# Cross-attention and feed-forward layer on one core: the sums' reciprocals on VectorE, the softmax's high part one step later, the last eight groups divided ahead too

## The chip, the cores and the metric

The kernel runs on one core of one Trainium2 chip. The metric is device time in microseconds (us) of one execution. The kernel before was timed three times: 1075.79, 1072.92 and 1074.25 us, median 1074.25 us. One more execution was recorded by the hardware profiler, and all rows below come from that one.

## The reference

Sixteen sequences of 128 tokens (2048 tokens, width 1024) pass through one cross-attention layer and one gated feed-forward layer, all in float32:

```python
x = x + xattn(layernorm(x), ctx, ctx, w_q, w_k, w_v, w_out, mask)
x = x + ffn(layernorm(x), w12, b12, w3, b3)

# xattn: 32 query heads of 32 columns, 8 key/value groups (4 query heads share one group)
scores = einsum('bghnd,bgsd->bghns', query, key) / 32 ** 0.5
scores = where(mask, scores, finfo.min)
out = einsum('bghns,bgsd->bghnd', softmax(scores), value) @ w_out.T

# ffn
x1, x2 = split(x @ w12.T + b12)
y = (silu(x1) * x2) @ w3.T + b3
```

## The kernel before

**Pieces.** TensorE multiplies 16-bit numbers, so each float32 operand is split into a high float16 part (written by ScalarE, `*_hi`) and a low part, the rest (written by VectorE or GpSimd, `*_lo`). A product is three matmuls: high by high, high by low, low by high. The engines are named in the profile as PE (TensorE), ACT (ScalarE), DVE (VectorE), POOL (GpSimd) and SP (the queue that issues the DMAs). Each engine runs its instructions strictly in the order in which they are written, and waits on semaphores.

**Blocks, steps and groups.** The 16 sequences are taken as 8 blocks of U = 2 sequences, and the attention of a block as 8 key/value groups. A group g = 0 to 63 is thus one key/value group of one pair of sequences: 8 score tiles of 128 by 128 (u = 0, 1 and four heads j each). The main loop is `for t in 1..8, for s in 0..7`: step (t, s) works on group g = 8(t-1)+s, and every engine has a loop of that shape of its own. Beside the group, a step holds a unit or two of other work: the q, k and v projections of block t, the turning (transposing) of the next x rows at s = 7, the output projection of block t-2 at s = 3 to 6, the splitting of the next block's context on POOL at s = 0 and 1 (`split_ctx`, L928), the look at later weights' maxima on DVE (`max_of`, L1729). At t = 8 the first feed-forward products (`hidden`) and POOL's splitting of w12 take the place of the projections.

**A group's way.** PE: `scores(g)` (L1457). DVE: `mask_scores(g)` (L1884) adds the mask, finds each row's extreme and writes e, 8 instructions of L1895; after each four it counts up `neg_max_done`. ACT: `exps(g, u)` (L1201), four exponentials for each u. For a group in `NORMED` (8 to 47) they also leave each row's sum in p_sum, and P is divided by its sums before it is split: by DVE for the two first groups of a block (`by_vector`, L308; `norm_prob` in the DVE program, L1908: a reciprocal L1912 and a product L1915 for each u), by POOL for the other six (`by_pool`, L313; `norm_prob` of POOL, L975: a scaling L979, a power of -1 L981 and a product L985 for each u). Then ACT writes the high part of both u in one instruction (`prob_hi`, L1213, L1222), POOL the low part in two (`prob_lo`, L969, L972; in groups outside 12 to 47 the u = 0 half is DVE's, L1903). SP turns both parts with a DMA transpose (`turn_prob`, L727), and PE multiplies them with v (`weigh`, L1474) three steps after the scores. For groups in NORMED that is the tiled form (L1487 to L1493): 32 columns of v as weights, four heads side by side in the array, and the result is already transposed. For the other groups (0 to 7 and 48 to 63) P is not divided, `weigh` runs two steps after the scores in the plain form (L1497 to L1501) with a column of ones that gives the sum, DVE divides the result (`divide`, L1920) and PE turns it (`turn_attn`, L1424).

**What ties the steps.** e is kept for two groups only (index g % 2). So `mask_scores(g)` waits (L1890 to L1893) until both parts of group g-2 are split, and `scores(g+1)` waits until `mask_scores(g)` has read its bank (L1465). Products go through five PSUM banks in turn (three at the beginning and end), and each product waits until the bank's last content was read (`begin`, L1381). In the order before, ACT's step is `exps(g, 0)`, the high parts of the step's first unit and of the attention result g-3, `exps(g, 1)`, the second unit's high part, `prob_hi(g)` (L1309 to L1339). POOL's step is `prob_lo(g-1)`, `norm_prob(g)`, then its splits (L990 to L1007). DVE's step is L2082 to L2127.

## Time and profile before

| quantity | value |
|---|---|
| time, median of 3 | 1074.25 us |
| the profiled execution's own time | 1076.37 us |
| its span, first to last instruction | 1074.6 us |
| PE busy | 1026.1 us (95%) |
| DVE busy | 670.4 us (62%) |
| POOL busy | 644.7 us (60%) |
| ACT busy | 473.2 us (44%) |
| mean granted clock of PE, share of 2.4 GHz | 0.979 |

1.8 us of the profiled execution lie outside its span. A busy share is an average over all stages: the attention takes about the first 600 us, the feed-forward products the rest. The profile counts a matmul busy until its modelled end, and matmuls overlap, so what a group of short matmuls costs is read from start to start. "PEclk" 1.00 is 2.4 GHz and 0.50 is 1.2 GHz. A row of idle time such as "[3.10 <-ACT arena_rows L1298]" says how long the engine had waited before that instruction and whose work ended the wait.

### The profile page before, as it was taken

How to read it: one execution, taken by the hardware profiler on the slowest of the kernel's cores; microseconds unless marked ns; L12 is line 12 of the kernel's file. 1: busy time of each engine (PE TensorE's matmuls, PEld its weight loads, DVE VectorE, ACT ScalarE, POOL GpSimd, SP SyncE). 2: the span in 40 equal slices, each digit the busy share in tenths (PEclk: the TensorE clock that was granted, in tenths of full speed). 3: DMA queues.
4: the chain of work that ended last, by engine and by line, in shares of the span. 5: the costliest groups of instructions: out<-in, count | busy, mean ns of one | idle time of the engine just before them, and what ended most of it. 6: DMA issues, size and time to landing. Idle time of an engine off the chain costs nothing.

```text
span 1074.6 us, 22142 instructions
## 1 busy us (share of the span) xinstructions
PE 1026.1 (95%) x8320; PEld 683.5 (64%) x8320; DVE 670.4 (62%) x2040; ACT 473.2 (44%) x1303; POOL 644.7 (60%) x657
## 2 busy tenths in 40 slices
PE   8898899998979989989999999999999999999998
PEld 7786757766658557677755544444444788468853
DVE  6889976767677667777856523735766255635431
ACT  5767566656566556666566511123432011301110
POOL 2769877987978879878985879226862201203000
PEclk8998999998999989989999999999999999999999
DMA  9569676897798788969994552397649731774201
GB/s 370 212 171 190 152 193 166 175 249 198 193 219 217 206 210 176 254 173 237 231 255 79 136 218 94 134 271 255 225 164 226 267 113 55 196 238 135 80 30 49
DMA packets 230779, 199.13 MB, mean 185 GB/s; under 512 B 177040, under 2 KB 187280, under 8 KB 225808
## 3 DMA queue, kind: packets, MB, share of 16 engines
q1 hardware_dynamic: 230672, 197.72, 67.1%
q8 instruction: 66, 1.08, 0.4%
q14 instruction: 41, 0.34, 0.1%
HBM read 119.04 MB, written 35.65 MB: 144 GB/s over the span
## 4 chain that ended last, share of the span: by engine, by line
PE 61%; POOL 19%; ACT 5%; DVE 4%; issue 4%; DMA 1%; SPq 1%; DVEq 0%; POOLq 0%; ACTq 0%
PE bank_dense L1411 38%; PE bank_spare L1411 7%; PE bank_score L1567 6%; PE bank_spare L1567 5%; POOL arena_attn L972 5%; POOL arena_attn L981 4%; POOL arena_attn L985 4%; PE bank_av L1567 3%; POOL arena_in L908 2%; ACT arena_attn L1207 2%; POOL arena_in L904 2%; ACT arena_attn L1222 2%; DVE arena_attn L1895 1%; POOL arena_in L906 1%; PE bank_score L1468 1%
## 5 line engine op out<-in xcount | busy, mean ns | idle before, releaser
L1411 PE MATMUL bank_dense<-arena_rows,arena_in 128*128 128x256 f16 (+1 forms) x1272 | 176.1, 296 | 1.6 <-POOL arena_in L908 0.9
L1411 PE MATMUL bank_dense<-arena_attn,arena_rows 128*128 128x512 f16 x768 | 166.4, 379 | 0.0
L1411 PEld LDWEIGHTS bank_dense<-arena_rows,arena_in 128*128 128x128 f16 x1272 | 122.1, 98 | 44.5 <-DVE arena_in L1743 1.3
L1895 DVE CUSTOM_DVE_ANT_0 arena_attn<-bank_score,arena_in 128x128 f32<-128x128 f32 x512 | 143.5, 344 | 0.7 <-PE bank_score L1468 0.5
L1411 PEld LDWEIGHTS bank_dense<-arena_attn,arena_rows 128*128 128x128 f16 x768 | 75.2, 98 | 90.1
L972 POOL TENSOR_TENSOR arena_attn<-arena_attn 128x512 f16<-128x512 f32 x89 | 103.3, 1177 | 46.8 <-ACT arena_attn L1222 46.8
L1207 ACT ACTIVATE arena_attn<-arena_attn,arena_in 128x128 f32<-128x128 f32 x320 | 123.7, 390 | 16.5 <-DVE arena_in L1895 16.5
L1411 PE MATMUL bank_dense<-arena_out,arena_attn 128*128 128x512 f16 x576 | 127.8, 379 | 0.5 <-DVE arena_attn L1937 0.5
L1222 ACT ACTIVATE arena_attn<-arena_attn 128x1024 f16<-128x1024 f32 x64 | 67.5, 1055 | 108.5 <-POOL arena_attn L985 96.8
L1411 PEld LDWEIGHTS bank_dense<-arena_out,arena_attn 128*128 128x128 f16 x576 | 55.5, 98 | 64.0 <-DVE arena_attn L1937 0.6
L1411 PE MATMUL bank_spare<-arena_rows,arena_in 128*128 128x256 f16 (+1 forms) x648 | 87.7, 292 | 0.0
L1411 PE MATMUL bank_dense<-arena_out,arena_in 128*128 128x512 f16 x384 | 83.0, 379 | 0.0
L908 POOL TENSOR_TENSOR arena_in<-arena_in 128x512 f16<-128x512 f32 x62 | 77.1, 1243 | 5.0
L1210 ACT ACTIVATE arena_attn<-arena_attn,arena_in 128x128 f32<-128x128 f32 x192 | 60.8, 391 | 34.1 <-DVE arena_in L1895 33.8
L1411 PEld LDWEIGHTS bank_spare<-arena_rows,arena_in 128*128 128x128 f16 x648 | 62.3, 98 | 19.8
L2000 DVE SCALAR_TENSOR_TENSOR arena_out<-bank_dense,small,arena_out 128x256 f32<-128x256 f32 x64 | 27.9, 478 | 74.9 <-PE bank_dense L1411 74.9
L1411 PEld LDWEIGHTS bank_dense<-arena_out,arena_in 128*128 128x128 f16 x384 | 37.6, 98 | 45.3
L1411 PE MATMUL bank_dense<-arena_in 128*128 128x256 f16 x456 | 64.4, 308 | 1.5 <-DVE arena_in L1750 1.4
L985 POOL TENSOR_TENSOR arena_attn<-arena_attn 128x512 f32<-128x512 f32 x60 | 62.4, 1039 | 4.7
L981 POOL TENSOR_TENSOR arena_attn<-arena_attn 128x4 f32<-128x4 f32 x60 | 62.1, 1035 | 5.0
L918 POOL TENSOR_TENSOR small<-small 128x1 f32<-128x1 f32 x32 | 20.2, 633 | 72.9 <-DVE small L1784 72.9
L1207 ACT ACTIVATION_READ_ACCUMULATOR arena_attn<-arena_attn,arena_in 128x1 f32 x320 | 60.6, 189 | 0.0
(237 smaller groups left out, 1942.1 us busy)
## 6 DMA issues: line engine op xcount, KB each, us to landing
arena_rows<-x SPq DMA_DIRECT2D x32, 512.0 KB, 5.4
arena_in<-w_scratch SPq DMA_DIRECT2D x64, 256.0 KB, 3.0
arena_attn<-q_scratch SPq DMA_DIRECT2D x48, 256.0 KB, 4.3
arena_rows<-w_t SPq DMA_DIRECT2D x12, 1024.0 KB, 6.4
arena_rows<-ctx_t SPq DMA_DIRECT2D x8, 1024.0 KB, 5.9
q_scratch<-arena_attn SPq DMA_DIRECT2D x16, 512.0 KB, 4.6
x_scratch<-arena_rows SPq DMA_DIRECT2D x16, 512.0 KB, 4.1
arena_out<-x_scratch SPq DMA_DIRECT2D x16, 512.0 KB, 5.7
```

The source lines that it names most:

```text
L904: pool.tensor_tensor(buf, src, spread, ALU.mult).then_inc(s_pool, 1)
L908: pool.tensor_tensor(lo, buf, hi, ALU.subtract).then_inc(ready, 1)
L972: ins = pool.tensor_tensor(p_split[:, g % 2, u, 1], e[:, g % 2, u], p_split[:, g % 2, u, 0], ALU.subtract)
L981: pool.tensor_tensor(inv_pool[:, u], inv_pool[:, u], minus_one.broadcast_to([P, HPG]), ALU.pow)\
L985: ins = pool.tensor_tensor(heads, heads, inv_pool[:, u].rearrange("p (j o) -> p j o", o=1) .broadcast_to([P, HPG, SEQ]), ALU.mult)
L1207: ins = act.activation(head, head, ACT.Exp, bias=neg_max[:, g % 2, h:h + 1], scale=-1.0, accum_out=p_sum[:, g % 2, u, j:j + 1])
L1210: ins = act.activation(head, head, ACT.Exp, bias=neg_max[:, g % 2, h:h + 1], scale=-1.0)
L1222: act.activation(p_split[:, g % 2, :, 0], e[:, g % 2], ACT.Copy).then_inc(s_phi, 1)
L1411: ins = pe.matmul(dst, lhs(a, c), rhs(b, c), start=(c == chunks[0] and n == 0), stop=(c == chunks[-1] and n == 2))
L1567: ins = pe.matmul(seven(v, j), weights[:, a, P * c:P * c + P], rows[:, b, c], start=(c == 0 and n == 0), stop=(c == 3 and n == 2))
L1895: ins = dve.tensor_tensor_reduce(out=e[:, g % 2, h // HPG, SEQ * (h % HPG):SEQ * (h % HPG) + SEQ], in0=B_SCORE[:, SEQ * h:SEQ * h + SEQ], ...
L2000: ins = dve.scalar_tensor_tensor(out=cols, in0=bank("y", f, q)[:, 256 * k:256 * k + 256], scalar=c_ffn[:, 2 * h + k:2 * h + k + 1], in1=co ...
```

## The change

Four things change.

1. The reciprocals of all divided groups are made by DVE, in a new helper `inv_sums(g, u)`: a scaling of p_sum by 1/P_SCALE and a reciprocal, each on 128 by 4 numbers and with a wait between them. POOL's `norm_prob(g, u)` is only the product. Where DVE divides, its own product becomes a `tensor_tensor` behind the same two small instructions.
2. For POOL's groups the second half's reciprocal, the second half's product and the high part move to the next step: DVE calls `inv_sums(g-1, 1)` at the start of step g ahead of `mask_scores(g)`, POOL's step is `norm_prob(g-1, 1)`, `prob_lo(g-1)`, `norm_prob(g, 0)`, and ACT calls `prob_hi(g-1)` behind `exps(g, 0)`.
3. Groups 56 to 63 join NORMED, all divided by DVE. At t = 8 DVE's `norm_prob(g)` stands ahead of `first_half_read` and `attn_lo`.
4. With that, groups 56 to 63 are weighed in the tiled form, three steps behind their scores, and lose `divide` and `turn_attn`.

```diff
-NORMED = range(8, 48)
+NORMED = [*range(8, 48), *range(56, 64)]

 def by_vector(g):
-    return g in NORMED and g % GROUPS < 2
+    return g in NORMED and (g % GROUPS < 2 or g >= 56)

 def by_pool(g):
-    return g in NORMED and g % GROUPS >= 2
+    return g in NORMED and g % GROUPS >= 2 and g < 56

+def inv_count(g, u):
+    return U * normed_count(g - 1) + u + 1
...
# POOL
-            def norm_prob(g):
+            def norm_prob(g, u):
                 n = normed_count(g - 1, by_pool)
-                for u in range(U):
-                    pool.wait_ge(s_exp, 2 * g + u + 1)
-                    pool.tensor_scalar(inv_pool[:, u], p_sum[:, g % 2, u], 1 / P_SCALE, None, ALU.mult).then_inc(s_pinv, 1)
-                    pool.wait_ge(s_pinv, 2 * (U * n + u) + 1)
-                    pool.tensor_tensor(inv_pool[:, u], inv_pool[:, u], minus_one.broadcast_to([P, HPG]), ALU.pow)\
-                        .then_inc(s_pinv, 1)
-                    pool.wait_ge(s_pinv, 2 * (U * n + u) + 2)
-                    heads = e[:, g % 2, u].rearrange("p (j n) -> p j n", j=HPG)
-                    ins = pool.tensor_tensor(heads, heads, inv_pool[:, u].rearrange("p (j o) -> p j o", o=1)
-                                             .broadcast_to([P, HPG, SEQ]), ALU.mult)
-                ins.then_inc(s_pnorm, 1)
+                pool.wait_ge(s_vinv, inv_count(g, u))
+                heads = e[:, g % 2, u].rearrange("p (j n) -> p j n", j=HPG)
+                pool.tensor_tensor(heads, heads, inv[:, g % 2, u].rearrange("p (j o) -> p j o", o=1)
+                                   .broadcast_to([P, HPG, SEQ]), ALU.mult).then_inc(s_pnorm, 1)
...
-                    if GROUPS * (t - 1) + s > PLO_ALONE:
-                        prob_lo(GROUPS * (t - 1) + s - 1)
-                    if by_pool(GROUPS * (t - 1) + s):
-                        norm_prob(GROUPS * (t - 1) + s)
+                    g = GROUPS * (t - 1) + s
+                    if by_pool(g - 1):
+                        norm_prob(g - 1, 1)
+                    if g > PLO_ALONE:
+                        prob_lo(g - 1)
+                    if by_pool(g):
+                        norm_prob(g, 0)
...
# ACT
                     exps(g, 0)
+                    if by_pool(g - 1):
+                        prob_hi(g - 1)
...
-                    prob_hi(g)
+                    if not by_pool(g):
+                        prob_hi(g)
...
# PE, the steps behind the loop
-                turn_attn(NG - 11 + s)
-                if s < 10:
-                    weigh(NG + s - 10)
+                weigh(NG - 11 + s)
...
# DVE
+            def inv_sums(g, u):
+                dve.wait_ge(s_exp, 2 * g + u + 1)
+                dve.tensor_scalar(sums[:, g % 2, u], p_sum[:, g % 2, u], 1 / P_SCALE, None, ALU.mult).then_inc(s_vsum, 1)
+                dve.wait_ge(s_vsum, inv_count(g, u))
+                dve.reciprocal(inv[:, g % 2, u], sums[:, g % 2, u]).then_inc(s_vinv, 1)
...
                 for u in range(U):
-                    dve.wait_ge(s_exp, 2 * g + u + 1)
-                    dve.reciprocal(inv_vector[:, u], p_sum[:, g % 2, u]).then_inc(s_vinv, 1)
-                    dve.wait_ge(s_vinv, U * n + u + 1)
+                    inv_sums(g, u)
+                    dve.wait_ge(s_vinv, inv_count(g, u))
                     heads = e[:, g % 2, u].rearrange("p (j n) -> p j n", j=HPG)
-                    ins = dve.scalar_tensor_tensor(out=heads, in0=heads, scalar=P_SCALE,
-                                                   in1=inv_vector[:, u].rearrange("p (j o) -> p j o", o=1)
-                                                   .broadcast_to([P, HPG, SEQ]), op0=ALU.mult, op1=ALU.mult)
+                    ins = dve.tensor_tensor(heads, heads, inv[:, g % 2, u].rearrange("p (j o) -> p j o", o=1)
+                                            .broadcast_to([P, HPG, SEQ]), ALU.mult)
...
+                    if by_pool(g - 1):
+                        inv_sums(g - 1, 1)
                     if g >= 3:
                         divide(g - 3)
                     mask_scores(g)
...
+                    if by_vector(g) and t == NB:
+                        norm_prob(g)
                     if t == NB and s in H_AT:
                         first_half_read(0, H_AT[s])
                     if g >= 3:
                         attn_lo(g - 3)
-                    if by_vector(g):
+                    if by_vector(g) and t < NB:
                         norm_prob(g)
+                    elif by_pool(g):
+                        inv_sums(g, 0)
```

What stands in a row on POOL at step s = 3 of block t = 4 (group 27) before: L972 is `prob_lo(26)`, L979, L981 and L985 are `norm_prob(27)`, L918 and L925 are small work for a row's scale.

```order
L972 TENSOR_TENSOR arena_attn<-arena_attn 128x512 [waits prob_hi_done]
L972 TENSOR_TENSOR arena_attn<-arena_attn 128x512
L979 TENSOR_SCALAR arena_attn<-arena_attn 128x4 [waits exp_done]
L981 TENSOR_TENSOR arena_attn<-arena_attn 128x4 [waits pool_inv_sum_done]
L985 TENSOR_TENSOR arena_attn<-arena_attn 128x512 [waits pool_inv_sum_done]
L979 TENSOR_SCALAR arena_attn<-arena_attn 128x4 [waits exp_done]
L981 TENSOR_TENSOR arena_attn<-arena_attn 128x4 [waits pool_inv_sum_done]
L985 TENSOR_TENSOR arena_attn<-arena_attn 128x512 [waits pool_inv_sum_done]
L918 TENSOR_TENSOR small<-small 128x1 [waits var_done]
L925 TENSOR_TENSOR arena_in<-arena_in,small 128x1 [waits root_done]
```

And now (L980 is the product, L973 `prob_lo(26)`, L921 and L928 the small work):

```order
L980 TENSOR_TENSOR arena_attn<-arena_attn 128x512 [waits inv_sum_of_prob_done]
L973 TENSOR_TENSOR arena_attn<-arena_attn 128x512 [waits prob_hi_done]
L973 TENSOR_TENSOR arena_attn<-arena_attn 128x512
L980 TENSOR_TENSOR arena_attn<-arena_attn 128x512 [waits inv_sum_of_prob_done]
L921 TENSOR_TENSOR small<-small 128x1 [waits var_done]
L928 TENSOR_TENSOR arena_in<-arena_in,small 128x1 [waits root_done]
```

Four small instructions are gone, and the second product of group 26 stands ahead of its low part.

ACT at the same place before, from the end of step s = 2 through step 3 (L1207 an exponential, L1222 `prob_hi`, L1177 the attention result's high part, L1191 that of k):

```order
L1222 ACTIVATE arena_attn<-arena_attn 128x2x512 [waits even_prob_turned,prob_normed_by_pool]
L1207 ACTIVATE arena_attn<-arena_attn,arena_in 128x128 [waits neg_max_done]
L1207 ACTIVATE arena_attn<-arena_attn,arena_in 128x128 x3
L1177 ACTIVATE arena_attn<-bank_dense2 128x256 [waits dense_done]
L1207 ACTIVATE arena_attn<-arena_attn,arena_in 128x128 [waits neg_max_done]
L1207 ACTIVATE arena_attn<-arena_attn,arena_in 128x128 x3
L1191 ACTIVATE arena_in<-bank_spare 128x256 [waits dense_done,k_spilled_0]
L1222 ACTIVATE arena_attn<-arena_attn 128x2x512 [waits odd_prob_turned,prob_normed_by_pool]
```

And now (L1204, L1219, L1174 and L1188 are the same):

```order
L1204 ACTIVATE arena_attn<-arena_attn,arena_in 128x128 [waits neg_max_done]
L1204 ACTIVATE arena_attn<-arena_attn,arena_in 128x128 x3
L1219 ACTIVATE arena_attn<-arena_attn 128x2x512 [waits even_prob_turned,prob_normed_by_pool]
L1174 ACTIVATE arena_attn<-bank_dense2 128x256 [waits dense_done]
L1204 ACTIVATE arena_attn<-arena_attn,arena_in 128x128 [waits neg_max_done]
L1204 ACTIVATE arena_attn<-arena_attn,arena_in 128x128 x3
L1188 ACTIVATE arena_in<-bank_spare 128x256 [waits dense_done,k_spilled_0]
L1204 ACTIVATE arena_attn<-arena_attn,arena_in 128x128 [waits neg_max_done]
```

`prob_hi(26)` stood ahead of the first exponentials of group 27; now it stands behind them and ahead of the attention result's high part. `prob_hi(27)` is no longer in this step.

DVE at step s = 4 of t = 8 (group 60), between two runs of `mask_scores`, before (L1905 `prob_lo`, L1952 the output projection's sum, L1937 the attention result's low part, L1925 and L1927 `divide`):

```order
L1895 ISA arena_in 128x1
L1895 ISA arena_attn,arena_in<-bank_score,arena_in 128x128
L1895 ISA arena_in 128x1
L1895 ISA arena_attn,arena_in<-bank_score,arena_in 128x128
L1895 ISA arena_in 128x1
L1895 ISA arena_attn,arena_in<-bank_score,arena_in 128x128
```

And now (L1908, L1910 and L1917 are the scaling, the reciprocal and the product for each u, L1903, L1953 and L1935 as L1905, L1952 and L1937 before):

```order
L1893 ISA arena_in 128x1
L1893 ISA arena_attn,arena_in<-bank_score,arena_in 128x128
L1893 ISA arena_in 128x1
L1893 ISA arena_attn,arena_in<-bank_score,arena_in 128x128
L1893 ISA arena_in 128x1
L1893 ISA arena_attn,arena_in<-bank_score,arena_in 128x128
L1893 ISA arena_in 128x1
L1893 ISA arena_attn,arena_in<-bank_score,arena_in 128x128
L1893 ISA arena_in 128x1
L1893 ISA arena_attn,arena_in<-bank_score,arena_in 128x128
```

Six instructions, two of them on 512 columns, stand where `divide` had two.

## Rows read from the trace of the kernel before

**Rows 1.** DVE by line and shape: busy us, mean ns | idle before.

```profile
L1731 DVE TENSOR_REDUCE arena_in<-arena_rows 128x1 f32<-128x2048 f32 x19 | 43.3, 2279 | 14.5 <-DMA arena_rows<-w_t 14.5
```

**Rows 2.** Busy time by engine, PEclk, DMA; stretches t = 2, 3, 4, 7, and 8 (s = 3 to 6).

```profile
112.90:185.30 72.40, 65.53 (x646) 46.99 (x642) 55.96 (x202) 42.99 (x162) 56.36 (x63) 0.98 0.67 164
185.30:256.80 71.50, 65.56 (x660) 46.76 (x661) 49.66 (x190) 43.18 (x163) 59.89 (x68) 0.95 0.87 214
256.80:328.40 71.60, 65.64 (x661) 46.80 (x661) 49.75 (x190) 43.20 (x163) 59.87 (x68) 0.95 0.84 209
...
471.60:539.20 67.60, 67.13 (x712) 50.66 (x713) 54.10 (x227) 42.39 (x106) 59.48 (x64) 1.00 0.90 220
...
574.10:599.90 25.80, 25.80 (x239) 14.59 (x236) 19.67 (x89) 13.90 (x37) 18.10 (x19) 1.00 0.48 103
```

**Rows 3.** The chain that ended last, 255 to 327 us: start, us, what.

```profile
284.50 2.28 POOL arena_attn L972 x2
...
287.17 1.05 POOL arena_attn L981
...
288.29 1.04 POOL arena_attn L985
...
291.90 1.07 ACT arena_attn L1222
...
293.03 2.27 POOL arena_attn L972 x2
```

**Rows 4.** Who waited for whom, whole span: us in total, times, longest.

```profile
ACT arena_attn L1222 <- POOL arena_attn L985: 96.8, 25, 6.7
...
POOL arena_attn L972 <- ACT arena_attn L1222: 46.8, 32, 6.8
```

**Rows 5.** PE's instructions in order of time at t = 3, s = 7: start, us, [idle before].

```profile
248.53 0.66 PE L1420 MATMUL bank_spare<-arena_in,arena_rows 128*128 128x128 f32 x4 [3.10 <-ACT arena_rows L1298]
250.80 1.12 PE L1420 MATMUL bank_spare<-arena_in,arena_rows 128*128 128x128 f32 x4 [1.61 <-DVE v_low L1865]
```

**Rows 6.** POOL by line and shape: busy us, mean ns | idle before.

```profile
L981 POOL TENSOR_TENSOR arena_attn<-arena_attn 128x4 f32<-128x4 f32 x60 | 62.1, 1035 | 5.0
...
L979 POOL TENSOR_SCALAR arena_attn<-arena_attn 128x4 f32<-128x4 f32 x60 | 14.0, 233 | 16.4 <-ACT arena_attn L1207 13.2
```

**Rows 7.** DVE in order of time, t = 4: the first instruction of `mask_scores(24)` to (27).

```profile
257.94 0.35 DVE L1895 CUSTOM_DVE_ANT_0 arena_attn<-bank_score,arena_in 128x128 f32<-128x128 f32 x1
...
264.49 0.33 DVE L1895 CUSTOM_DVE_ANT_0 arena_attn<-bank_score,arena_in 128x128 f32<-128x128 f32 x1
...
271.53 0.33 DVE L1895 CUSTOM_DVE_ANT_0 arena_attn<-bank_score,arena_in 128x128 f32<-128x128 f32 x1
...
279.55 0.34 DVE L1895 CUSTOM_DVE_ANT_0 arena_attn<-bank_score,arena_in 128x128 f32<-128x128 f32 x1
```

**Rows 8.** DVE's small instructions in SBUF: duration min/median/max, ns.

```profile
L1880 DVE TENSOR_SCALAR arena_in<-arena_in,small x8: 221/223/1187, 60.8 to 539.6; 128x8 f32<-128x8 f32 x8
```

**Rows 9.** The same view of the reciprocal.

```profile
L1912 DVE RECIPROCAL arena_attn<-arena_attn x20: 159/168/178, 120.6 to 412.9; 128x4 f32<-128x4 f32 x20
```

**Rows 10.** DVE in order of time at t = 8, s = 6.

```profile
596.79 1.68 DVE L1905 TENSOR_TENSOR arena_attn<-arena_attn 128x512 f16<-128x512 f32 x1
```

**Rows 11.** POOL in order of time, the same moment.

```profile
596.76 1.16 POOL L908 TENSOR_TENSOR arena_in<-arena_in 128x512 f16<-128x512 f32 x1
```

**Rows 12.** The chain that ended last, 110 to 186 us: tiled `weigh`, four exponentials with sums.

```profile
152.40 0.45 PE bank_dense L1489 x24
...
180.60 1.54 ACT arena_attn L1207 x8
```

**Rows 13.** PE in order of time, t = 8: `turn_attn`, the first plain `weigh` matmul, `scores(63)`.

```profile
599.11 0.38 PE L1428 MATMUL bank_dense<-arena_in 128*128 128x128 f32 x2
599.33 0.18 PE L1497 MATMUL bank_av<-v_high,arena_attn 128*128 128x33 f16 x1
...
599.94 0.61 PE L1468 MATMUL bank_score<-arena_attn 96*128 96x128 f16 x8
```

More of the change, by code:

```diff
@@ L433, in xattn_ffn @@
         p_sum = part(arena_attn, 59, 1, F32)[:, 0:2 * U * HPG].rearrange("p (r u j) -> p r u j", r=2, u=U)
-        inv_pool = part(arena_attn, 60, 1, F32)[:, 0:U * HPG].rearrange("p (u j) -> p u j", u=U)
-        minus_one = part(arena_attn, 62, 1, F32)[:, 0:1]
-        inv_vector = part(arena_attn, 61, 1, F32)[:, 0:U * HPG].rearrange("p (u j) -> p u j", u=U)
+        sums = part(arena_attn, 60, 1, F32)[:, 0:2 * U * HPG].rearrange("p (r u j) -> p r u j", r=2, u=U)
+        inv = part(arena_attn, 61, 1, F32)[:, 0:2 * U * HPG].rearrange("p (r u j) -> p r u j", r=2, u=U)
         k_stack = part(arena_attn, 63, 4).rearrange("p (b g n) -> p b g n", b=2, g=4)
@@ L1214, in prob_hi @@
                 if by_pool(g):
-                    act.wait_ge(s_pnorm, normed_count(g, by_pool))
+                    act.wait_ge(s_pnorm, U * normed_count(g, by_pool))
                 elif by_vector(g):
```

8 lines of the change are left out of this document (2 added, 6 removed).

## The prediction

> **What bounds the kernel now.** The page's busy times, which stand in the table above, come first: PE is busy 1026.1 of 1074.6 us, so all that PE idles is 48.5 us. Then the busy times by block [rows 2]: blocks t = 3 to 6 take 71.5 or 71.6 us each (two of the four are shown, the others read alike), with PE busy 65.6 of them at a mean clock of 0.95. So PE idles 6.0 us in each, and 0.05 of lost clock is about 7 us at 1.2 GHz, whose busy part costs 2.6 to 3.4 us. A block in which PE never waited would take 71.6 - 6.0 - (2.6 to 3.4) = 62.2 to 63.0 us, and I take 62.6. What PE waits for is in the chain [rows 3]: it runs through POOL, not PE. In one step the low part of the group before (2.28 us, from 284.50), then twice the scaling, the power (1.05) and the product (1.04) with a wait of about 0.07 between them, then ACT's high part (1.07), then POOL's next low part at 293.03. That is 8.53 us a step, of which none can run beside another: POOL waits for ACT and ACT for POOL. The waits say the same from both sides [rows 4]: ACT sat 96.8 us until POOL's product, POOL 46.8 us until ACT's high part. PE's steps s = 3 to 6 last about as long, but at s = 0 to 2 PE is faster and POOL's two context splits slower, and the debt is paid at s = 7, where PE waits 3.10 us for an x row that ACT scaled too late (it stood behind `prob_hi`) and 1.61 us for v's low part behind the exponentials [rows 5]. The clock dips follow these waits.
>
> **What goes.** For each of 30 groups POOL loses two powers of 1.035 us and two scalings of 0.233 us [rows 6], with their waits 2.8 us a step, and ACT's 1.07 us leaves the loop since POOL no longer needs the high part of its own group in the same step. POOL is busy 59.9 us of a block [rows 2]; less 6 x 2 x 1.27 = 15.2 it is 44.7. POOL stops being a bound, except that at s = 0 and 1 its splits (two trios of instructions a step, some 6.7 us) still hold up the low part by which `mask_scores` two groups on is released.
>
> **What comes in its place: DVE and its ping-pong with ACT.** DVE now makes 12 pairs in a block for POOL's groups and four scalings for its own. The reciprocal has one price, 0.17 us [rows 9]. The scaling has none in the rows for 128 by 4; the nearest is L1880, a scaling of 128 by 8 in SBUF: 0.22 us in the median and 1.19 at most [rows 8]. The long ones began while POOL was at work. The same is seen at 596.79: DVE's subtraction from SBUF took 1.68 us, begun while POOL's L908 ran from 596.76 for 1.16 us, and so ended about half a microsecond after it [rows 10, 11]. So a scaling costs 0.25 to 1.2 us, a pair 0.45 to 1.4. Below 0.45 nothing speaks for it. I take 0.45 where POOL is waiting for this very pair (most second halves) and 0.8 to 0.9 elsewhere.
>
> The Trainium skill ("SBUF — State Buffer", Terms) says that DVE and GpSimd arbitrate for one port pair, and that "the loser fully blocks"; "GPSIMD Engine Reference" (Specifications) narrows it to DVE instructions in a two-port mode or with two SBUF inputs. The trace agrees: 1.68 us beside 1.16 us, and a reciprocal never above 0.178 us. By this rule the scaling was the wrong instruction to hand to DVE in s = 0 and 1, where POOL splits without a gap; the high end above is what it would give.
>
> Now the chain of DVE through a block, from the start of one `mask_scores` to the next. Before, it was 6.55, 7.04 and 8.02 us for s = 0 to 3 [rows 7], back to back. Now:
> - s 0 to 1: 6.55 + 0.96 (ACT's high part of group 7 of the block before now stands between the exponentials and all that DVE waits for, 1.07 less overlap [rows 3]) + two scalings, and a first product that meets POOL: 8.0 to 9.6, I take 9.0.
> - s 1 to 2: 7.04 + two scalings: 7.5 to 9.4, take 8.1.
> - s 2 to 3: 8.02 + two pairs: 8.9 to 10.8, take 9.2.
> - s 3 to 7, four intervals: none was back to back before. The interval 2 to 3 holds half of the mask, four exponentials (1.54 [rows 12]), the high and low parts behind them, a maximum (L1731, 2.28 us [rows 1]) and a row's statistics; steps 3 to 6 have only one of these two last. So 8.02 less about 2, plus the high part 0.96 and two pairs of 0.45 (to 0.9 for one): 6.9 to 7.9 without the low part that now waits behind the attention result (L1934, 0.3 to 0.4 more). I take 7.9 each, 31.6; 7.2 and 8.3 are the ends.
> - s 7 to 0: the same with four x halves, gather and block scales: 9.6 to 10.6, take 10.
> The sum is 34.0 + 28.8 = 62.8 at the low ends, 36.3 + 31.6 = 67.9 as taken, 40.4 + 33.2 = 73.6 at the high ends. PE's floor of 62.6 lies at or below all of them: the step is bound by DVE and ACT in turn. Since the takes lean to contention, and POOL is idle a third of the time, I set the block at 66.8, a little below the taken sum. That is 71.6 - 66.8 = 4.8 us, and in four blocks 19.2 us. PE then waits some 4 us a block in pieces of at most 2 us; block t = 2 lost 6.9 us of PE's time with a mean clock of 0.98 [rows 2], so I expect most of the dips to go.
>
> **Block t = 2** (72.4 us) is already DVE's at its first three steps: DVE is busy 56.0 us in it against 49.7 later [rows 2]. There each scaling lands on the path: 4 x 0.6 and two pairs, 3.5 us more; its s = 7 gets about 1.5 us shorter. Net +2.
>
> **Block t = 7** (67.6, PE busy 67.1) is PE's own and stays.
>
> **Block t = 8.** The tiled form costs 0.45 us a group [rows 12]. The plain one costs 599.94 - 599.33 = 0.61 and the turn 599.33 - 599.11 = 0.22 [rows 13], together 0.83. Saved: 8 x 0.38 = 3.0 us, since PE is the bound there (25.8 of 25.8 us at s = 3 to 6 [rows 2]). That PE's busy column gives far more to the plain form is only overlap. Against it: DVE at s = 3 to 6. It is busy 19.7 of 25.8 us, 4.9 a step [rows 2]. It loses `divide` (about 0.65) and gains two scalings, two reciprocals and two products of 512 columns, 0.7 to 1.3 each: 2 x (0.25 + 0.2 + 0.7) = 2.3 to 2 x (0.7 + 0.2 + 1.25) = 4.3. DVE's step becomes 6.6 to 8.6 us, against PE's 6.45 - 0.38 = 6.07. POOL splits w12 there nearly without gaps, so I take 8.3. `scores(g+1)` waits for `mask_scores(g)`, which now stands behind the products of group g-1: the first such wait is about 1, the next two 2.2 each, 5.4 us. Net +2.4, say +2. At s = 0 to 2 and 7 a step is over 11 us and hides it. The DMA transposes get a step more time.
>
> **Sum.** 1076.4 - 19.2 + 2 + 0 + 2 = 1061.2 for the profiled execution. It was 2.1 us above the median of the runs, so the same difference of -15.2 gives 1059.0 us.
>
> **Rivals.**
> - *DVE's additions stay hidden and PE is the bound.* For it: DVE was busy only 49.7 of 71.6 us, and its waits for ACT could absorb 12 pairs. Against: DVE's intervals at s = 0 to 3 were already back to back. Blocks of 63.5: -32; t = 2 at 0, t = 8 at 0: 1043. Chance 0.25.
> - *POOL and ACT keep the pace.* The low parts at s = 0 and 1 still stand behind the splits, the high part costs ACT's time ahead of each attention result, and blocks end at 69.5 us: -8.4 + 2 + 2: 1070. Chance 0.15.
> - *DVE becomes a worse bound than POOL was: slower.* One mechanism: each scaling and product waits for POOL's running instruction. If a pair costs 1.2 us on average instead of my 0.45 to 0.9, the 12 pairs alone add 4 to 6 us to the 67.9, its chain is 72, PE's waits at s = 7 stay over 3 us and the dips with them. It decides from a mean of about 1.2 us a pair; the price is +0.5 a block, +5 at t = 2, +6 at t = 8: 1074.25 + 2 + 5 + 6 = 1087. The skill's rule above is what would make it so. Against: POOL waits for the pair in most steps, and then its port is free. Chance 0.11.
> - *The change does not do what it says.* The order shows that the power and scalings are gone from POOL and the high part moved, so only its timing is open: 0.04, no change.
>
> **How the numbers follow.** The forecast has 0.45. Its own range, with blocks of 65 to 68.5, is 1051 to 1067. Down to 1040 it takes in most of the first rival, up to 1073 the second and a little of the third. This kernel can be told from no change at 0.3%, 3.2 us. Faster than 1071.0: 0.45 + 0.25 + 0.13 of the second = 0.83. Slower than 1077.5: 0.10 of the third. Within: the rest, 0.02 + 0.01 + 0.04 = 0.07.
>
> **What would show it.** Right: blocks t = 3 to 6 of 65 to 68.5 us; POOL busy about 45 in each; ACT's wait for POOL's product nearly gone and DVE's waits for ACT's high parts grown; scalings of 0.2 to 1.2 us, mean 0.4 to 0.6; PE's waits now for `mask_scores` (L1893) at s = 2 to 4 and for low parts at s = 7; PEclk 0.99 or 1.00 there; at t = 8, s = 3 to 6, a step of 7.5 to 8.5 us, ended by `mask_scores`. Wrong: blocks under 64 (DVE hid it), blocks over 70 with POOL's low part ahead of each `mask_scores` (second rival), or a mean pair over 1.2 us (third).

## The result and the profile after

The changed kernel takes 1114.59 us (median of 4 runs, 1113.54 to 1117.02) against 1074.65 us before: 1.0376 times as long, 95% interval 1.0354 to 1.0399. I had forecast 1059.0. It is slower, on the other side of no change, and 41.6 us beyond the range's upper end of 1073.

The profiled executions differ by 1115.2 - 1074.6 = 40.6 us of span. By the starts of `scores` the difference lies here: block t = 2 +0.3 us; blocks t = 3 to 6, 77.6, 78.3, 78.2 and 76.4 instead of 71.5 or so, +24.2 together; block t = 7 +3.8; from the start of t = 8 to the end 547.8 instead of 535.4, +12.4. Busy times of the whole, the granted clock in 40 slices, and the chain by engine:

```profile
PE 1036.3 (93%) x8304; PEld 679.9 (61%) x8304; DVE 734.9 (66%) x2212; ACT 478.2 (43%) x1367; POOL 571.3 (51%) x536
...
PEclk8999899898898989999999999999999999999999
...
PE 52%; DVE 20%; ACT 7%; DMA 7%; issue 4%; POOL 3%; SPq 2%; ACTq 0%; DVEq 0%; POOLq 0%
```

The same by stretches, as in [rows 2]: t = 2, 3, 5, 7, and t = 8 from s = 4 on.

```profile
112.70:185.50 72.80, 66.03 (x649) 47.51 (x644) 60.28 (x229) 43.03 (x162) 40.08 (x39) 0.95 0.60 149
185.50:263.10 77.60, 68.87 (x661) 47.66 (x661) 58.81 (x219) 43.21 (x163) 44.41 (x44) 0.91 0.79 199
341.40:419.60 78.20, 68.18 (x660) 47.41 (x659) 58.74 (x218) 43.02 (x163) 44.39 (x44) 0.91 0.76 192
496.00:567.40 71.40, 67.69 (x714) 50.75 (x714) 54.73 (x229) 42.06 (x106) 60.01 (x65) 1.00 0.90 220
612.00:650.00 38.00, 31.96 (x266) 15.16 (x265) 35.84 (x107) 19.81 (x80) 25.91 (x25) 0.91 0.37 84
```

POOL's column did what was forecast: 44.4 us a block where it was 59.9. But no engine of these blocks is full. PE idles 8.7 us of block t = 3 and 10.0 of t = 5, and its clock is 0.91 in both, not the 0.99 that I expected. At t = 8 it is DVE that is full: 35.8 of 38.0 us. Who waited for whom, as in [rows 4], and in a second fence DVE's maxima with the idle time before them, as in [rows 1]:

```profile
POOL arena_attn L973 <- ACT arena_attn L1219: 101.8, 37, 7.5
...
POOL arena_attn L980 <- DVE arena_attn L1910: 77.3, 31, 7.9
...
ACT arena_attn L1219 <- DVE arena_attn L1917: 55.7, 18, 4.6
```

```profile
L1729 DVE TENSOR_REDUCE arena_in<-arena_rows 128x1 f32<-128x2048 f32 x19 | 43.1, 2270 | 24.2 <-DMA arena_rows<-w_t 24.2
```

ACT's wait for POOL's product, 96.8 us in [rows 4], is gone; POOL now waits for DVE's reciprocal instead. And DVE stands 24.2 us in front of its maxima until a load of weights has landed, where it stood 14.5 before. The chain of waits shows what that means. At t = 5, from step 5 into step 7:

```profile
393.71 0.96 ACT arena_attn L1219
394.74 2.28 POOL arena_attn L973 x2
397.07 1.79 SPq L736
398.92 7.14 DMA arena_rows<-w_t
406.08 2.29 DVE arena_in L1729
408.37 0.33 DVE arena_attn L1863
408.96 0.35 DVE arena_attn L1893
```

Read it downwards: P's high part, one step late, lets POOL make the low parts; these release SyncE's transpose of P (L736); only behind that does SyncE's queue issue the load of the next weights, 7.14 us; then DVE takes their maximum, and behind that in its row stand what `mask_scores` (L1893) and all of the next step need. The same place in SyncE's queue, step 3 of t = 5, after and (second fence) before the change; the blocks begin at 341.4 and 328.4 us, so the context load leaves 38.4 us into the block instead of 33.0, and the weight load right behind it:

```profile
366.98 12.72 SPq L736 DMA_TRANSPOSE arena_attn<-arena_attn  x2
379.75 0.57 SPq L698 DMA_DIRECT2D arena_rows<-ctx_t  x1
380.38 0.42 SPq L760 DMA_DIRECT2D arena_rows<-w_t  x1
```

```profile
349.86 11.49 SPq L733 DMA_TRANSPOSE arena_attn<-arena_attn  x2
361.41 0.57 SPq L695 DMA_DIRECT2D arena_rows<-ctx_t  x1
362.04 0.42 SPq L757 DMA_DIRECT2D arena_rows<-w_t  x1
```

### The profile page after: what moved, and what is told of

The parts are those of the page before. It is cut to its first block, busy times and chain, and to the rows that moved or that the text cites. A ratio compares the mean times of both kernels' runs of the same rounds, so it can differ in the third digit from the quotient of the medians.

```text
span 1115.2 us, 22218 instructions
## 1 busy us (share of the span) xinstructions
PE 1036.3 (93%) x8304; PEld 679.9 (61%) x8304; DVE 734.9 (66%) x2212; ACT 478.2 (43%) x1367; POOL 571.3 (51%) x536
## 4 chain that ended last, share of the span: by engine, by line
PE 52%; DVE 20%; ACT 7%; DMA 7%; issue 4%; POOL 3%; SPq 2%; ACTq 0%; DVEq 0%; POOLq 0%
PE bank_dense L1411 33%; PE bank_score L1567 5%; PE bank_spare L1567 5%; DVE arena_attn L1893 5%; PE bank_spare L1411 5%; DMA arena_rows<-w_t 5%; ACT arena_attn L1204 4%; PE bank_av L1567 3%; DVE arena_in L1729 2%; DVE arena_attn L1908 2%; DVE arena_attn L1917 2%; POOL arena_attn L973 2%; SPq L736 2%; DVE arena_attn L1903 1%; DVE arena_attn L1863 1%
## 5 line engine op out<-in xcount | busy, mean ns | idle before, releaser
L1204 ACT ACTIVATE arena_attn<-arena_attn,arena_in 128x128 f32<-128x128 f32 x384 | 148.8, 391 | 129.0 <-DVE arena_in L1893 129.0
L1411 PE MATMUL bank_dense<-arena_rows,arena_in 128*128 128x256 f16 (+1 forms) x1272 | 180.2, 300 | 1.8 <-POOL arena_in L911 1.0
L973 POOL TENSOR_TENSOR arena_attn<-arena_attn 128x512 f16<-128x512 f32 x89 | 102.9, 1173 | 101.8 <-ACT arena_attn L1219 101.8
L1893 DVE CUSTOM_DVE_ANT_0 arena_attn<-bank_score,arena_in 128x128 f32<-128x128 f32 x512 | 143.8, 346 | 1.4 <-PE bank_score L1468 0.8
L1411 PE MATMUL bank_dense<-arena_out,arena_attn 128*128 128x512 f16 x576 | 136.1, 396 | 4.4 <-DVE arena_attn L1935 4.4
L1411 PEld LDWEIGHTS bank_dense<-arena_out,arena_attn 128*128 128x128 f16 x576 | 57.3, 101 | 74.9 <-issue 10.9
L980 POOL TENSOR_TENSOR arena_attn<-arena_attn 128x512 f32<-128x512 f32 x60 | 63.3, 1055 | 77.3 <-DVE arena_attn L1910 77.3
L1219 ACT ACTIVATE arena_attn<-arena_attn 128x1024 f16<-128x1024 f32 x64 | 67.1, 1048 | 55.8 <-DVE arena_attn L1917 55.7
L911 POOL TENSOR_TENSOR arena_in<-arena_in 128x512 f16<-128x512 f32 x62 | 77.9, 1256 | 5.0
L1204 ACT ACTIVATION_READ_ACCUMULATOR arena_attn<-arena_attn,arena_in 128x1 f32 x384 | 72.7, 189 | 0.0
L1411 PE MATMUL bank_dense<-arena_in 128*128 128x256 f16 x456 | 59.4, 293 | 1.5 <-DVE arena_in L1748 1.4
L921 POOL TENSOR_TENSOR small<-small 128x1 f32<-128x1 f32 x32 | 19.9, 622 | 78.7 <-DVE small L1782 78.7
L1468 PE MATMUL bank_score<-arena_attn 96*128 96x128 f16 x512 | 40.1, 222 | 20.8 <-DVE arena_in L1893 19.4
L1729 DVE TENSOR_REDUCE arena_in<-arena_rows 128x1 f32<-128x2048 f32 x19 | 43.1, 2270 | 24.2 <-DMA arena_rows<-w_t 24.2
```

The costliest lines, as they stand in the source:

```text
L911: pool.tensor_tensor(lo, buf, hi, ALU.subtract).then_inc(ready, 1)
L973: ins = pool.tensor_tensor(p_split[:, g % 2, u, 1], e[:, g % 2, u], p_split[:, g % 2, u, 0], ALU.subtract)
L980: pool.tensor_tensor(heads, heads, inv[:, g % 2, u].rearrange("p (j o) -> p j o", o=1) .broadcast_to([P, HPG, SEQ]), ALU.mult).then_inc(s_ ...
L1204: ins = act.activation(head, head, ACT.Exp, bias=neg_max[:, g % 2, h:h + 1], scale=-1.0, accum_out=p_sum[:, g % 2, u, j:j + 1])
L1219: act.activation(p_split[:, g % 2, :, 0], e[:, g % 2], ACT.Copy).then_inc(s_phi, 1)
L1411: ins = pe.matmul(dst, lhs(a, c), rhs(b, c), start=(c == chunks[0] and n == 0), stop=(c == chunks[-1] and n == 2))
```

## The experiments

Before was measured anew beside each group of kernels: 1073.9 to 1075.3 us. All times are medians; a kernel's "gain" is against the changed kernel's 1114.6.

**Loads first.** In SyncE's steps:

```
+ if 3 <= t < 7 and s == 3: load_look(look_at(t, 4), w3_t[t - 3])
+ if 3 <= t < 7 and s == 5: load_look(look_at(t, 6), w12_t[2 * (t - 3) + 1])
+ if t < NB - 1 and s == 3: load_ctx(t + 1)
  if g >= 1: turn_prob(g - 1)
  ...
- (the same three, from behind turn_prob)
```

> The changed kernel with one thing moved in SyncE's order: at steps 3 and 5 of blocks 3 to 6 the loads of the weights that VectorE takes maxima of (L760 in the changed kernel), and at step 3 the load of the next context (L698), are issued ahead of that step's transposes of P instead of behind them. Theory A (VectorE's row of work is the bound of every block from 2 on, and 5.4 to 6.6 us of it a block are waits of L1729 for these loads, which leave late because the transposes ahead of them in SyncE's queue wait for the P low parts that now come later): the waits of L1729 fall from 24.2 us in all to under 8, the two long intervals between the starts of mask_scores (12.2 to 13.3 us from step 4 to 5, 10.0 to 10.4 from step 6 to 7) fall to 8 to 9, blocks 3 to 6 from 78 to 72 or 73 us, the whole to 1090 to 1096 us. Theory B (the wait only stands where another would stand: POOL's second product, the matmul rows at half clock, or a transfer that isn't faster for leaving earlier): under 6 us gained, 1109 to 1115 us.

1091.01 us, 1.0159 of before (1.0135 to 1.0184): a gain of 23.6 us. L1729's wait for weights is 0.6 us in all, and blocks 3 to 6 take 70.6, 72.0, 71.3 and 72.1 us, a little below theory A's 72 or 73. Theory A holds. The edit moves the context load too, but no engine of the changed kernel waits for one, so the gain is that of the loads for the maxima. By place: blocks 3 to 6 are 24.4 us shorter, block t = 7 is 1.7 longer. Block t = 5 in four stretches, s = 0 to 2, 3, 4 to 6, 7:

```profile
326.80:348.60 21.80, 19.08 (x242) 16.06 (x241) 18.61 (x73) 12.32 (x48) 16.83 (x16) 1.00 0.85 224
348.60:361.20 12.60, 11.89 (x80) 6.28 (x81) 10.63 (x35) 6.99 (x32) 7.79 (x10) 0.73 0.96 277
361.20:387.70 26.50, 26.50 (x244) 16.30 (x243) 20.80 (x80) 16.08 (x60) 15.08 (x16) 1.00 0.83 189
387.70:398.10 10.40, 8.90 (x100) 7.38 (x98) 8.35 (x33) 8.29 (x26) 4.75 (x5) 1.00 0.60 148
```

The third row matters for the forecast: in steps 4 to 6 PE is busy 26.50 of 26.50 us at full clock. It needs 8.8 us for each of these steps, whatever DVE does. Most of what the block loses, it loses in steps 0 to 3: DVE's intervals of 8.9 us hold up `scores` at the start of step 3 by 2.5 us and the output projection behind it by 0.7, and then PE runs at a clock of 0.73 through step 3:

```profile
348.59 0.94 PE L1468 MATMUL bank_score<-arena_attn 96*128 96x128 f16 x8 [2.52 <-DVE arena_in L1893]
350.24 7.96 PE L1411 MATMUL bank_dense<-arena_out,arena_attn 128*128 128x512 f16 x24 [0.71 <-DVE arena_attn L1935]
```

**The last groups as before.** `NORMED` is again `range(8, 48)`, and behind the loop `turn_attn` and `weigh` as before the change.

> The changed kernel with groups 56 to 63 as before the change (no product on P, division after the weighting, turned attention); the rest of the change stays. It prices the part on groups 56 to 63. Theory A (its price is paid in block 8 alone: steps 3 to 6 there are set by VectorE at 9.5 us instead of TensorE's 6.45, and at step 3 TensorE waits 3.6 us for ScalarE, which stands behind VectorE's products): from the start of block 8 to the end the kernel comes back from 547.8 us to 535 to 538, the whole to 1101 to 1105 us. Rival (block 8 is late because the seven blocks before hand it a late start for its operands, whatever its groups do): the end part stays at 545 or more and the whole above 1111 us.

1102.75 us (1.0269, 1.0247 to 1.0290): a gain of 11.8. From the start of t = 8, at 565.0, to the end at 1100.4 it is 535.4 us again. Theory A holds. Blocks 3 to 6 stay at 76.2 to 78.3. The part on groups 56 to 63 costs what the end part lost. Where: DVE's row in step 5 of t = 8 of the changed kernel, and (second fence) POOL at that time.

```profile
621.12 1.02 DVE L1908 TENSOR_SCALAR arena_attn<-arena_attn 128x4 f32<-128x4 f32 x1
622.18 0.18 DVE L1910 RECIPROCAL arena_attn<-arena_attn 128x4 f32<-128x4 f32 x1
622.39 1.40 DVE L1917 TENSOR_TENSOR arena_attn<-arena_attn 128x512 f32<-128x512 f32 x1
623.71 0.57 DVE L1908 TENSOR_SCALAR arena_attn<-arena_attn 128x4 f32<-128x4 f32 x1
624.32 0.18 DVE L1910 RECIPROCAL arena_attn<-arena_attn 128x4 f32<-128x4 f32 x1
624.53 1.51 DVE L1917 TENSOR_TENSOR arena_attn<-arena_attn 128x512 f32<-128x512 f32 x1
```

```profile
620.96 1.16 POOL L911 TENSOR_TENSOR arena_in<-arena_in 128x512 f16<-128x512 f32 x1
622.20 1.04 POOL L907 TENSOR_TENSOR arena_in<-arena_in,small 128x512 f32<-128x512 f32 x1
623.31 0.95 POOL L909 CAST arena_in<-arena_in 128x512 f16<-128x512 f32 x1
624.34 1.15 POOL L911 TENSOR_TENSOR arena_in<-arena_in 128x512 f16<-128x512 f32 x1
```

The first scaling, of 128 by 4 numbers, ends at 622.14; POOL's L911 had ended at 622.12. The second ends at 624.28, POOL's L909 at 624.26. Each product ends 0.55 us after the POOL instruction that ran when it began. Two pairs and two products take 4.9 us here (621.12 to 626.04), so DVE's step is 9.5 us where PE needs 6.2 (step 4, in which it does not wait). At step 3 the products also hold up ACT, whose high part, table load and SiLU stand before the attention result that the output projection needs:

```profile
605.94 7.04 PE L1411 MATMUL bank_spare<-arena_out,arena_attn 128*128 128x512 f16 x24 [3.65 <-DVE arena_attn L1938]
```

After 3.65 us of idling the 24 matmuls run partly at the lower clock: 7.04 us, where the same 24 take 5.35 in the next step. The granted clock of the whole step is 0.85.

**No scaling.** In `inv_sums` the `tensor_scalar` goes and the reciprocal reads `p_sum`; the kernel leaves out the factor of 1/P_SCALE.

> The changed kernel without the scaling of the sums by 1/16384 (VectorE L1908 goes, 0.51 us a piece, 8.1 us a block by its 16); the reciprocals are taken of the sums themselves, so P goes into the weighting without its factor of 16384 and the output is too small by it in groups 8 to 47 and 56 to 63. The work is otherwise the same. Theory A (VectorE's row is the bound of blocks 2 to 6, so what leaves it leaves the block): 12 of the 16 pairs of a block stand in it at 0.5 us or more with a gap of 0.07, so blocks 3 to 6 lose 6 to 9 us each, block 2 some 3 to 5, block 8 some 4; the whole 1076 to 1086 us. Rival (the waits for the loads and for ScalarE fill what is freed): blocks lose 3 us or less, the whole 1098 to 1110 us.

1087.79 us (1.0125, 1.0104 to 1.0146): a gain of 26.8, near theory A but beyond its 1086 on the slow side. By place it is not as A had it: blocks 3 to 6 fall by only 3.1 to 4.6 us each, 14.9 together, and L1729's wait for weights grows to 35.4 us. DVE is earlier, SyncE's queue isn't, so part of the gain is handed to the loads. The end part, from 547.8 to 534.8, gave 13.0 where A had 4.

**Products in their own step.** GpSimd calls `norm_prob(g, 0)` and `norm_prob(g, 1)` behind `prob_lo(g - 1)`, ScalarE calls `prob_hi(g)` at the end of each step, VectorE `inv_sums(g, 1)` last in it.

> The changed kernel with the one-step delay undone and the reciprocals left on VectorE: GpSimd makes both products of a group in that group's step, ScalarE takes P's high part at the end of that step, VectorE makes the second reciprocal as the last thing of the step (the same place in its row but for one small instruction). Theory A (the delay matters only through what waits for P's low part: SyncE's transposes, and the loads behind them): the low parts come 2 to 4 us earlier in a step, the waits of L1729 for the loads fall from 24 us to 8 to 15, and the whole comes to 1095 to 1107 us. Theory C (the delay is what freed ScalarE: without it ScalarE waits for GpSimd's second product, which itself waits for VectorE's last instruction, and the exponentials of the next step stand behind that): blocks 3 to 6 grow by 3 us or more each, the whole 1125 us or more.

1102.06 us (1.0258, 1.0233 to 1.0283): a gain of 12.5. The loads' wait is 13.7 us, blocks 3 to 6 take 74.9 to 75.4. Theory A; C falls, though ACT again waits 94.4 us for POOL's product.

**Sums at stride 2.** `p_sum` and `sums` become `...[:, 0:4 * U * HPG]` rearranged with a last dimension of 2, of which element 0 is used.

> The changed kernel with the sums of P and the scaled sums laid out at every second element (stride 2) instead of side by side; nothing else differs. In the changed kernel the scaling L1908 of 128x4 numbers takes 0.16 us where GpSimd is idle and up to 1.12 us beside it, 0.51 us in the mean, while the reciprocal L1910 of the same size takes 0.17 to 0.18 us everywhere. Theory P (the scaling waits only because a contiguous tensor_scalar runs in a form that shares a port with GpSimd; spread elements take it out of that form): the scalings take 0.15 to 0.25 us each, blocks 3 to 6 lose 4 to 6 us each, the whole 1092 to 1101 us. Rival (the wait is that of any multiplication beside GpSimd, whatever its layout): the mean stays at 0.45 us or more, the whole 1110 to 1118 us.

1118.47 us (1.0416, 1.0394 to 1.0438): no gain, 3.9 us worse, and the cause stays open: blocks t = 3 to 5 read as in the changed kernel, but t = 6 takes 78.1 us instead of 76.4 and t = 7 74.2 instead of 71.4. The 66 scalings that begin while POOL works still take 0.64 us in the mean. So the wait is not one of the layout's side-by-side elements. The Trainium skill ("VectorE: DVE Perf Modes", What auto-detection actually checks) asks for unit steps only in the mode for 16-bit tensors, not in the two-port mode of a single source in SBUF; by that rule stride could change nothing, and the run agrees.

**A second reciprocal in the scaling's place.**

```
- dve.tensor_scalar(sums[:, g % 2, u], p_sum[:, g % 2, u], 1 / P_SCALE, None, ALU.mult).then_inc(s_vsum, 1)
+ dve.reciprocal(sums[:, g % 2, u], p_sum[:, g % 2, u]).then_inc(s_vsum, 1)
...
- dve.reciprocal(inv[:, g % 2, u], sums[:, g % 2, u]).then_inc(s_vinv, 1)
+ dve.reciprocal(inv[:, g % 2, u], p_sum[:, g % 2, u]).then_inc(s_vinv, 1)
```

The first result is not used, and the factor of 1/P_SCALE is left out.

> The changed kernel with each scaling of the sums on VectorE replaced by a second reciprocal of the same 128x4 numbers, with the same wait behind it; the count of VectorE's instructions, their order and their semaphores are unchanged, and P goes into the weighting without its factor of 16384 in groups 8 to 47 and 56 to 63. It tells the instruction apart from what it waits for. Theory P (a reciprocal doesn't stand still for GpSimd's running instruction, as L1910 doesn't at 0.18 us everywhere, and the scaling does, at 0.51 us in the mean): all of the new first instructions take 0.18 us, so 16 x 0.33 = 5.3 us a block leave VectorE's row; without the instruction and its gap (0.58 us a pair) the kernel measured 1087.8 us, 26.8 below the changed kernel, so this one gains 0.33/0.58 of that, some 15 us: 1094 to 1103 us. Rival N (the first VectorE instruction that touches these sums waits, whatever it is, or what is freed waits in the products that follow): the first reciprocal takes over 0.4 us in the mean, or the whole stays above 1108 us.

1095.57 us (1.0193, 1.0166 to 1.0220): a gain of 19.0, within theory P. Minimum, median and maximum of the new instruction, and of the scaling that it replaces:

```profile
L1908 DVE RECIPROCAL arena_attn<-arena_attn x96: 160/168/178, 118.6 to 628.5; 128x4 f32<-128x4 f32 x96
```

```profile
L1908 DVE TENSOR_SCALAR arena_attn<-arena_attn x96: 157/288/1145, 119.9 to 651.1; 128x4 f32<-128x4 f32 x96
```

Same size, same place, and 66 of the 96 begin while POOL works in both kernels: one never waits, the other up to a microsecond longer than alone. So it is the kind of instruction that waits, not the count of instructions. That what it waits for is a port is not shown by this run.

**The scaling on ScalarE.** VectorE's `tensor_scalar` goes; behind the exponentials of `exps(g, u)`:

```
+ act.wait_ge(s_exp, 2 * g + u + 1)
+ act.activation(sums[:, g % 2, u], p_sum[:, g % 2, u], ACT.Copy, scale=1 / P_SCALE).then_inc(s_vsum, 1)
```

> The changed kernel with the scaling of the sums by 1/16384 moved from VectorE to ScalarE, which does it as a copy right behind the exponentials; nothing is left out. In the changed kernel 66 of the 96 scalings on VectorE start while GpSimd works, take 0.63 us in the mean and end 0.02 to 0.03 us after the GpSimd instruction that was running; laying the sums out at stride 2 changed nothing. Theory P (VectorE stands still in such a scaling until GpSimd's instruction ends, ScalarE doesn't, and VectorE's row is the bound): 7 to 9 us a block leave VectorE's row, the copies on ScalarE take 0.2 to 0.3 us each and cost nothing of it, and the whole is within 5 us of the kernel without any scaling (1087.8 us), 1084 to 1093 us. Rival (what waited in the scaling waits elsewhere as soon as VectorE's row moves on, in the products or for ScalarE, which now makes the sums later): 1100 us or more.

1095.33 us (1.0196, 1.0175 to 1.0216): a gain of 19.3, between the two theories; 2 us outside P's bound. A copy takes 0.205 us on ACT, always; the 7.5 us that are missing against no scaling at all are not settled: DVE waits 6.8 us in all for these copies, and 33.8 for loads.

**Combinations.** Loads first and last groups as before, with stride 2 (which does nothing); then the same without the delay:

> The changed kernel with three edits together: the loads for the maxima ahead of the transposes in SyncE's order, groups 56 to 63 as before the change, and the sums at every second element; the one-step delay of P's high part and of the second product stays. The single edits measured 23.6 us (loads first) and 11.9 us (last groups). Theory A (VectorE's row is the bound in the blocks, and these three stretches lie one behind the other): 1114.6 - 23.6 - 11.9 - 15 to 20 = 1059 to 1064 us. Rival (with the loads out of the way another wait of the blocks, TensorE at half clock in step 3 above all, takes most of what the sums free, or the sums free nothing): 1070 to 1080 us.

> As the kernel of the three edits (loads first, last groups as before, sums at every second element), and the one-step delay undone as well: both products in the group's own step and P's high part at its end. Alone that was worth 12.5 us. Theory A (that gain came only through the loads' late start, which is gone here): within 3 us of the kernel that keeps the delay. Theory D (the delay also costs by itself, since P's low part and the weighting come later): 5 to 10 us below it. Theory C (once the loads are out of the way the delay helps, since ScalarE doesn't stand waiting for GpSimd): 4 us or more above it.

1079.46 us (1.0054, 1.0033 to 1.0075) and 1080.41 us (1.0064, 1.0045 to 1.0083). For the first, 1114.6 - 23.6 - 11.8 = 1079.2: the two gains add, the stride adds nothing, and the rival's number came out for a reason that the stride's run gives. The second is theory A: without the late loads the delay is worth nothing either way. That is a sum of two differences: without the delay block t = 6 is 2.4 us longer and t = 7 is 2.4 us shorter.

**Before, with loads first.** The same edit in the kernel before.

> The kernel before the change with the loads for the maxima ahead of the transposes in SyncE's order. There L1731 waits 14.5 us in all for these loads. Theory A (in the kernel before, GpSimd and ScalarE hold the pace and VectorE has room, so its waits for loads cost nothing): 1072 to 1077 us, within 0.3% of before. Rival (these loads cost time before the change too, so the 23.6 us they are worth in the changed kernel are not the change's): 1055 to 1068 us.

1074.68 us (1.0010, 0.9997 to 1.0022): theory A. There the late loads are covered, so their 23.6 us belong to the change.

**All three edits.** Loads first, last groups as before, scaling on ScalarE; with the delay, and without:

> The changed kernel with loads first, groups 56 to 63 as before the change, and the scaling on ScalarE; the one-step delay stays. Without the last edit (and with the stride, which did nothing) this measured 1079.5 us, with blocks of 71.3 to 72.8 us in which mask_scores starts follow at 9.1, 8.9 and 9.6 us in steps 0 to 2. Theory A (VectorE's row bounds these blocks): the three intervals fall by some 0.7 to 1.3 us each, TensorE's waits of 2.5 us and the half clock of step 3 behind them shrink, blocks come to 66 to 68 us, the whole to 1055 to 1063 us, which is faster than before the change. Rival (the blocks of 71 to 72 us have another floor in common with the kernel before, which three kernels of different order also show): blocks stay above 70 us and the whole at 1072 us or more.

> As the kernel with all three edits (loads first, last groups as before, scaling on ScalarE), with the one-step delay undone as well. Theory A (VectorE's row decides and the delay no longer matters once the loads leave early): within 4 us of it. Theory D (ScalarE now carries the copies too, and without the delay its wait for GpSimd's second product stands in the ring of VectorE, GpSimd and ScalarE): 5 us or more above it.

1066.80 us (0.9933, 0.9917 to 0.9948) and 1060.50 us (0.9876, 0.9856 to 0.9896): both faster than before the change, by less than 2%. The first misses its theory's 1063 by 4 us with blocks of 66.6 to 69.1; the second is better by 6.3 us, which neither theory had: once the loads leave early and DVE's row is shorter, the delay costs. In the traces 3.9 us of this are block t = 7 (69.2 instead of 73.0) and 3.0 are blocks 3 to 6; no run takes the two apart. The second kernel's blocks t = 4 and 5:

```profile
251.70:319.60 67.90, 64.77 (x660) 46.09 (x660) 51.09 (x202) 46.87 (x179) 44.60 (x44) 0.97 0.86 221
319.60:385.80 66.20, 63.08 (x660) 45.22 (x659) 50.56 (x202) 46.83 (x179) 44.60 (x44) 1.00 0.89 218
```

Blocks 3 to 6 are 67.4 us in the mean here, near the 66.8 us that I had forecast for the change. With the delay kept they are 68.2. Without the loads first they stay at 75.4 (the scaling on ScalarE alone), and without the scaling moved at 71.7 (the first combination). Of the four parts of the change this kernel keeps the first alone, DVE's reciprocals.

## Why the prediction was wrong

By the starts of `scores`, forecast and measured differ by 43.4 us in blocks 3 to 6 (-19.2, +24.2), by 10.4 from t = 8 on (+2, +12.4), by 3.8 at t = 7 and by -1.7 at t = 2.

*What bounds the kernel before* fits the runs: take POOL's powers and scalings away and mend what replaces them, and the block falls from 71.6 to between 66 and 69. *What goes* was right within 0.3 us (44.4 busy, 44.7 forecast).

*The price of a pair* was right in its mean: scalings of 16 x 0.51 us a block, with gap and reciprocal 0.7 a pair, forecast 0.45 to 0.9. The third rival's condition, a mean of 1.2 us, was not met. Yet the result has the third rival's sign and lies 28 us above its 1087: not by the pair's price.

*DVE's chain through the block* is where it failed. Forecast and measured intervals between the starts of `mask_scores` at t = 5, in the changed kernel and with loads first:

| interval | forecast | changed | loads first |
|---|---|---|---|
| s 0 to 1 | 9.0 | 9.07 | 9.1 |
| s 1 to 2 | 8.1 | 8.94 | 8.9 |
| s 2 to 3 | 9.2 | 9.59 | 9.6 |
| s 3 to 4 | 7.9 | 7.53 | 7.5 |
| s 4 to 5 | 7.9 | 12.83 | 8.0 |
| s 5 to 6 | 7.9 | 8.04 | 9.1 |
| s 6 to 7 | 7.9 | 10.07 | 9.2 |
| s 7 to 0 | 10 | 12.16 | 9.9 |
| sum | 67.9 | 78.2 | 71.3 |

Three steps of it failed. First, "I take 7.9 each" for the four intervals from s = 3 to 7: I followed what DVE does in them, and not what DVE waits for. SyncE works through its steps in order, and I did not follow that order past the moved low part: the transposes wait for P's low part, P's low part is a step later, and the loads for DVE's maxima are queued behind them. The row was there, 14.5 us of waits of L1731 for these loads [rows 1]; I used it for the duration of a maximum only. Of the 78.2 us this is 6.9 (78.2 - 71.3). The 7.9 was also too low by its own terms: 8.02 - 2 + 0.96 + 2 x 0.45 is 7.9 before the low part behind the attention result, and 8.2 to 8.7 with it and with the dearer pair.

Second, sums over a block were compared, DVE's 67.9 against PE's 62.6, as if the longer sum decided and PE's waits cost only themselves. With loads first, PE is busy 66.4 of the 71.3 us. Counted from the floor of 62.6, that is 4.9 us of waits, where I had 4.2, and 3.8 us by which the busy time is longer, for which I had nothing; 3.1 of them are step 3 at the lower clock (11.9 us busy, 8.8 needed). PE waits for DVE in steps 0 to 2 (19.1 us busy of 21.8), since `scores(g+1)` waits for `mask_scores(g)`; in steps 4 to 6 PE itself is full, at 8.8 us a step. DVE's four intervals from s = 3 to 7 come to 33.9 us, where I let them be 31.6. Third, the block was then set 1.1 us below the taken sum, for which no row spoke. The second and third together are 71.3 - 66.8 = 4.5 us a block, the first is 6.9. In the changed kernel itself PE idles 10.0 of the 78.2 us, and its busy time is 5.6 us over the floor.

*"Most of the dips go"* failed with it: the forecast had waits "in pieces of at most 2 us" and took them for harmless; with loads first one of 2.5 us came, and the step behind it took 12.6 us at a clock of 0.73 where PE needs 8.8. Such a wait of PE is paid twice.

*Block t = 2* was forecast at +2 (3.5 longer at first, 1.5 shorter at s = 7) and came at +0.3: its interval 0 to 1 is 3.1 us longer, and the interval 7 to 0 is 2.6 shorter. *Block t = 7* was forecast at 0 and came at +3.8: its step 1 holds statistics of rows that SyncE loads behind a transpose, and DVE waits 3.4 us for them (the kernel before doesn't wait there). It is the first step's mistake a second time. No edit was made on these loads alone, but the three kernels without the delay bear it out: this wait is 1.1 us or less in them, and the block takes 69.0 to 69.7 us instead of 71.4.

*Block t = 8* was forecast at +2.4, with DVE steps of 8.3 us and 5.4 us of waits. It costs 11.8 (the run with the last groups as before). The step was mis-sized: 9.5, since in steps 4 to 6 both products meet POOL (1.40 and 1.51 us where I took 0.7 to 1.25) as do both scalings (1.02 and 0.57), and P's low part as well (L1903, 1.45 us there, where three of the four low parts of these steps took 0.68 to 0.70 before the change). And steps 0 to 2 do not "hide it": in them DVE's products stand in a ring with ACT's high part and SiLU, by which step 3 is 5.2 us longer (11.68 against 6.45).

The rivals: the first (DVE hides it) is refuted, the second's 69.5 us a block was nearer than the forecast but for another reason, the third had the sign. None had SyncE's queue in it. The chance for slower, 0.10, was far too low for a change that moves work onto an engine whose intervals at s = 0 to 3 were back to back already, and makes a whole chain of releases one step later.

## What to carry to other kernels

When a result is produced a step later, follow it through every in-order queue that waits for it, the DMA issuer's above all, and ask what else stands behind it there: a load can be late for an engine that has nothing to do with the result. Compare the engines step by step and not by the larger of two sums, and price the lower clock behind each wait of the tensor engine. Adding the larger of each step overshoots too: it gives 27.6 + 4 x 8.8 + 9.9 = 72.7 us with loads first, where 71.3 was measured, and 70.0 against 66.2 in the last kernel's block t = 5. And hand to the vector engine, where GpSimd works beside it, an instruction that does not wait for GpSimd's, as the reciprocal here; this small scaling was better placed on the scalar engine, by 19.3 us.

## What the runs showed of the hardware

- A `tensor_scalar` of 128x4 numbers on VectorE takes 0.16 us alone. Of the 96 in the changed kernel 66 begin while a GpSimd instruction runs; 51 of these end 0.02 to 0.03 us after that instruction and take up to 1.14 us, and the mean of the 66 is 0.63. The other 15 take 0.16 us as well: 5 begin in the last 0.03 us of GpSimd's instruction, and 10 stand beside L921, an instruction of 128x1 numbers that takes 0.55 us. `reciprocal` of the same data takes 0.16 to 0.18 us in all 96 places; a scaled copy on ScalarE 0.205 to 0.208. The Trainium skill ("SBUF — State Buffer", Terms) has the lock held for the full instruction. The trace agrees for the 51, and in the other direction GpSimd's conversion L909 takes 0.61 us at 362.84 and 0.95 at 623.31, when VectorE's product was running; beside L921 it does not agree, and since the profile's spans on GpSimd are rough, the cause stays open. That a single-source instruction of only 4 numbers is locked as well I had priced and not expected to matter 96 times over: 19 to 27 us.
- The stride of such an operand changes nothing in this.
- A wait of TensorE of 2.5 us was followed by 12.6 us at a granted clock of 0.73 (between its levels of 1.2 and 2.4 GHz), one of 3.65 us by 24 matmuls in 7.04 us instead of 5.35.
